# Selective scan on VectorE: scans started from a constant, with a carry step of its own

## The reference, cut to what matters

```
delta = softplus(dts + dt_bias)            # per channel and token
for each token t, in order:                # h: channel x state
    dA = exp(delta[t] * A)                 # A negative, per channel and state
    h  = dA * h + (delta[t] * x[t]) * B[t] # B per state
    y  = sum over states of h * C[t]
out = y + D * x
```

## Time and profile before

| | |
|---|---|
| median of three runs | 24,350.81 us |
| span of the profiled execution | 24,349.2 us |
| time of the profiled execution | not given apart from its span; the fastest run took 24,349.69 us |
| VectorE busy | 23,408.4 us (96%) |
| TensorE busy | 23,475.9 us (96%) |
| ScalarE busy | 22,739.3 us (93%) |
| GpSimd busy | 20,766.4 us (85%) |
| scans in the trace | first start at 3,354.1 us, last at 23,661.3 us |

### The profile page before, as it was taken

One profiled execution on the slowest core, in us unless ns is written; L12 is line 12 of the kernel. 1 busy time (PEld: TensorE's weight loads), 2 busy tenths in 40 slices (PEclk: granted clock), 3 DMA queues, 4 the chain that ended last, 5 costly groups with the idle time before them and its releaser, 6 DMA issues. The chain is left out here.

```text
span 24349.2 us, 520057 instructions
## 1 busy us (share of the span) xinstructions
PE 23475.9 (96%) x197068; PEld 21113.9 (87%) x197068; DVE 23408.4 (96%) x23358; ACT 22739.3 (93%) x45975; POOL 20766.4 (85%) x6924
## 2 busy tenths in 40 slices
PE   5997989999999999999999999999999999999999
PEld 2775469999999999999999899999999999999987
DVE  7998889999999999999999999999999999999996
ACT  4996579999999999999999999999999999999986
POOL 3000049999999999999999999999999999999997
PEclk8998999999999999999999999999999999999999
DMA  5222555555555555555555566666655666666665
GB/s 191 59 64 96 185 184 188 188 186 189 188 186 188 182 189 188 188 190 189 188 188 188 189 193 195 196 194 195 196 194 190 192 199 193 193 198 194 193 200 189
DMA packets 3815249, 4429.59 MB, mean 182 GB/s; under 512 B 2085381, under 2 KB 3140521, under 8 KB 3532585
## 3 DMA queue, kind: packets, MB, share of 16 engines
q1 hardware_dynamic: 3812776, 4396.31, 55.2%
HBM read 3782.68 MB, written 617.09 MB: 181 GB/s over the span
## 5 line engine op out<-in xcount | busy, mean ns | idle before, releaser
L1475 DVE TENSOR_TENSOR_SCAN s_h<-s_da,s_h,s_db 128x512 f32<-128x512 f32 x16256 | 19189.5, 1273 | 86.9 <-PE s_db L1376 86.1
L1493 POOL TENSOR_TENSOR s_prod<-s_h,s_cb 128x2048 f32<-128x2048 f32 x4096 | 18660.9, 4572 | 357.9 <-DVE s_h L1475 289.6
L1445 ACT ACTIVATE s_da<-s_delta,a_neg 128x512 f32<-128x512 f32 x16384 | 10910.5, 718 | 27.0 <-DVE s_h L1475 0.8
L1434 ACT ACTIVATE s_dxb<-s_dx,s_btok 128x256 f32<-128x256 f32 x19328 | 8592.8, 505 | 30.7 <-PEq L63 30.7
L1389 PE MATMUL s_py<-eye,s_prod 128*128 128x128 f32 x65536 | 8498.0, 273 | 15.4 <-POOL s_prod L1493 15.4
L1376 PE MATMUL s_db<-s_bdiag,s_dx 128*128 128x128 f32 x49664 | 8226.6, 275 | 0.0
L1372 PE MATMUL s_db<-eye,s_dxb 128*128 128x128 f32 x40704 | 7232.2, 275 | 309.5 <-ACT s_dxb L1434 299.9
L1389 PEld LDWEIGHTS s_py<-eye,s_prod 128*128 128x128 f32 x65536 | 7435.7, 141 | 19.4 <-POOL s_prod L1493 19.2
L1376 PEld LDWEIGHTS s_db<-s_bdiag,s_dx 128*128 128x128 f32 x49664 | 6839.4, 191 | 0.0
L1372 PEld LDWEIGHTS s_db<-eye,s_dxb 128*128 128x128 f32 x40704 | 4926.4, 141 | 1380.1 <-issue 698.3
L546 POOL COPY a_spread<-a_rden 128x256 f32<-128x256 f32 x256 | 102.8, 402 | 1645.7 <-DVE a_rden L508 1645.7
(11 more groups left out here) (141 smaller groups left out, 16291.9 us busy)
## 6 DMA issues: line engine op xcount, KB each, us to landing
s_cb<-c_rows SPq DMA_DIRECT2D x2048, 1024.0 KB, 5.8
s_bdiag<-b_diag SPq DMA_DIRECT2D x2048, 256.0 KB, 4.9
s_bdiag<-b_diag SPq DMA_DIRECT2D x1536, 192.0 KB, 6.3
y<-s_yt SPq DMA_DIRECT2D x1024, 256.0 KB, 2.7
s_xc<-xc_own SPq DMA_DIRECT2D x384, 512.0 KB, 9.4
s_yb<-y SPq DMA_DIRECT2D x768, 256.0 KB, 4.0
xc_tok<-c_ot SPq DMA_DIRECT2D x32, 2048.0 KB, 7.6
s_xt<-xc_tok SPq DMA_DIRECT2D x256, 256.0 KB, 5.2
```

The costliest lines, as they stand in the source:

```text
L1434: last = e.activation(dxb[:, i % NDXB, j, :], dx[:, g % 2, j, :], ACT.Copy, scale=btok[:, g % 2, 0, j, n:n + 1])
L1445: last = e.activation(da[:, i % NDA, half, :], delta[:, g % 2, half, :], ACT.Exp, scale=wts[k]["a_neg"][:, half, n:n + 1])
L1475: last = e.tensor_tensor_scan(h[:, n, half, flow], da[:, i % NDA, half, flow], db[:, i % NDB, half, flow], first, ALU.mult, ALU.add)
L1493: e.tensor_tensor(prod[:, p % GROUPS_KEPT], h[:, states], columns.unsqueeze(2).to_broadcast([P, TOGETHER, HALVES, T]), ALU.mult).then_inc( ...
```

## The change

Each scan now starts from a constant: 1.0 in every tile but the first of a direction, where it is 0.0 as before. ScalarE writes the exponentials straight into `h` (the buffers `da` are gone), in all tiles but the first only for the 511 tokens after the first in the direction of the scan. VectorE writes the column that is left, by a step of its own (`carry`, a TENSOR_TENSOR of 128x16): the last column of the tile before times `fade`, the exponential of the first token, which ScalarE makes by two small instructions a tile. One carry serves eight states. The carry of states 0 to 7 for the tile to come stands after state 12, that of states 8 to 15 after state 4 of the tile itself.

Delta times x is done by VectorE in all directions (stage `dx`, from PSUM and `xt`), so GpSimd's `double` and ScalarE's copy are gone, and `xt` is loaded everywhere. In directions 2 and 3 `xc` is loaded for one half only. The scalings are shared out by two tables: `WHOLE` names the states with three scaled blocks (the others have two, with a second diagonal, in direction 1 now too), and `POOLED` those whose third block GpSimd scales.

```diff
-    NDA, NDXB, NDB = 3, 3, 2
+    NDXB, NDB = 3, 2
-    ADDED = {1: (5, 9), 2: (8, 11), 3: (8, 11)}
-    SKIPPED = 2
-    SHARE = 2
+    ADDED = {1: (5, 9), 2: (7, 11), 3: (7, 11)}
+    SKIPPED = 1
+    CARRIED = D_STATE // 2
+    CARRY_AT = {12: 0, 4: 1}
-    on_pool = lambda k, n, j: shared(k) and n % SHARE == SHARE - 1 and j == SUBS_ACT - 1
-    second_diagonal = lambda k, n: not shared(k) and n % GROUP != 0 and n != 6
-    scaled_subs = lambda k, n: SUBS_ACT - 1 if second_diagonal(k, n) else SUBS_ACT
+    WHOLE = {0: (0, 1, 4, 6, 8, 12, 15), 1: (0, 1, 2, 4, 6, 8, 10, 12, 14, 15),
+             2: (0, 3, 4, 6, 8, 10, 12, 14), 3: (0, 3, 4, 6, 8, 10, 12, 14)}
+    POOLED = {0: (4, 8, 12), 1: (2, 6, 10, 14), 2: (0, 4, 6, 10), 3: (0, 4, 6, 10)}
+    on_pool = lambda k, n, j: n in POOLED[k] and j == SUBS_ACT - 1
+    scaled_subs = lambda k, n: SUBS_ACT if n in WHOLE[k] else SUBS_ACT - 1
...
-        da = m.sb("s_da", [P, NDA, HALVES, T])
+        fade = m.sb("s_fade", [P, HALVES, D_STATE])
...
-            elif stage == "dx":
-                e.wait_ge(S["turnd"], n)
-                e.copy(flat(dx[:, s]), flat(pr[:, :, :])).then_inc(S["dx"], 1)
+            elif stage == "fade" and tile.t:
+                e.wait_ge(S["delta"], n)
+                if n >= 2:
+                    e.wait_ge(S["carry"], 2 * (n - 1))
+                for half in range(HALVES):
+                    last = e.activation(fade[:, half, :], wts[k]["a_neg"][:, half, :], ACT.Exp,
+                                        scale=delta[:, s, half, first_token(k):first_token(k) + 1])
+                last.then_inc(S["fade"], 1)
...
         PLAN_BACK = {
             "PE": {2: "dts", 9: "turnd"},
-            "ACT": {3: "exp", 4: "log", 10: "dx"},
-            "DVE": {5: "delta"},
-            "POOL": {3: "double"},
+            "ACT": {3: "exp", 5: "log", 7: "fade"},
+            "DVE": {6: "delta", 10: "dx"},
         }
...
-                        if i >= NDA:
-                            scanned(e, i - NDA, HALVES - 1)
+                        if g >= 1 and n % CARRIED == 0:
+                            e.wait_ge(S["carry"], 2 * (g - 1) + n // CARRIED + 1)
                         for half in range(HALVES):
-                            last = e.activation(da[:, i % NDA, half, :], delta[:, g % 2, half, :], ACT.Exp,
+                            last = e.activation(h[:, n, half, later(g)], delta[:, g % 2, half, later(g)], ACT.Exp,
                                                 scale=wts[k]["a_neg"][:, half, n:n + 1])
...
+                    def carry(g, part):
+
+                        if not 1 <= g < TILES:
+                            return
+                        states = slice(part * CARRIED, (part + 1) * CARRIED)
+                        if part == 0:
+                            e.wait_ge(S["fade"], g)
+                        multiplied(e, (g - 1) * D_STATE + (part + 1) * CARRIED - 1)
+                        e.tensor_tensor(h[:, states, :, first_token(k)], h[:, states, :, last_token],
+                                        fade[:, :, states].rearrange("p a n -> p n a"), ALU.mult).then_inc(S["carry"], 1)
+
...
-                        if g >= 1:
-                            multiplied(e, i - D_STATE)
                         for half in range(HALVES):
                             e.wait_ge(S["db"], 2 * i + half + 1)
-                            first = h[:, n, half, last_token:last_token + 1] if g else 0.0
-                            last = e.tensor_tensor_scan(h[:, n, half, flow], da[:, i % NDA, half, flow], db[:, i % NDB, half, flow],
-                                                        first, ALU.mult, ALU.add)
+                            last = e.tensor_tensor_scan(h[:, n, half, flow], h[:, n, half, flow], db[:, i % NDB, half, flow],
+                                                        1.0 if g else 0.0, ALU.mult, ALU.add)
                             last.then_inc(S["h"], 1)
+                        if n in CARRY_AT:
+                            carry(g if CARRY_AT[n] else g + 1, CARRY_AT[n])
                         for coming, stage in due("DVE", g, n):
                             prepare_dve(e, k, coming, stage)
```

More of the change, by code:

```diff
@@ L925, in scans_phase @@
                           "xst0 xst1 xld0 xld1 lowld btl0 btl1 bkeep "
-                          "turned xc proj low turnb btok dts exped log delta doubled turnd dx "
+                          "turned xc proj low turnb btok dts exped log delta fade carry turnd dx "
                           "scaled scaled_pool db da zero zeroed bstore bl0 bl1 bl2 bl3 h prod summed_first summed skipped added y0 y1")
@@ L960, in store_b @@
         def store_b(e, d, t, s):
-            for i in range(diagonals(d)):
+            for i in range(DIAGONALS):
                 there = b_diag[s, i].rearrange("(j m) -> j m", m=D_STATE * P + 1)[:, 0:D_STATE * P]
@@ L1032, in prepare_pe @@
                 e.wait_ge(S["delta"], n)
[L1033 to L1037, removed]
                 for j in range(SUBS):
@@ L1040, in prepare_pe, with first_token @@
                         at = (j % 2) * D_INNER + half * P
-                        last = e.transpose(pr[:, j // 2, at:at + P], source[:, half, j * P:(j + 1) * P], const["eye"][:, :])
+                        last = e.transpose(pr[:, j // 2, at:at + P], delta[:, s, half, j * P:(j + 1) * P], const["eye"][:, :])
                 last.then_inc(S["turnd"], 1)
+        def first_token(k):
+            return T - 1 if backwards(k) else 0
         def consumed(e, k, n):
@@ L1098, in prepare_dve @@
                 e.tensor_tensor(flat(dx[:, s]), flat(pr[:, :, :]), flat(xt[:, s]), ALU.mult).then_inc(S["dx"], 1)
[L1100 to L1105, removed]
         PLAN_KEPT = {
             "PE": {-2: "proj0", 0: "proj1", 3: "turnb", 5: "dts", 11: "turnd"},
-            "ACT": {1: "low", 6: "exp", 7: "log", 12: "dx"},
-            "DVE": {4: "btok", 8: "delta"},
-            "POOL": {4: "double"},
+            "ACT": {1: "low", 6: "exp", 7: "log", 9: "fade"},
+            "DVE": {4: "btok", 8: "delta", 12: "dx"},
         }
@@ L1114, in scans_phase @@
             "PE": {0: "proj0", 1: "proj1", 3: "turnb", 5: "dts", 11: "turnd"},
-            "ACT": {2: "low", 6: "exp", 7: "log", 12: "dx"},
-            "DVE": {4: "btok", 8: "delta"},
-            "POOL": {4: "double"},
+            "ACT": {2: "low", 6: "exp", 7: "log", 9: "fade"},
+            "DVE": {4: "btok", 8: "delta", 12: "dx"},
         }
@@ L1186, in one_direction, with later @@
             last_token = 0 if backwards(k) else T - 1
+            def later(g):
+                if g == 0:
+                    return slice(0, T)
+                return slice(0, T - 1) if backwards(k) else slice(1, T)
             def prepares(g):
@@ L1288, in load_own @@
                             e.wait_ge(S["dx"], t - 2)
-                        e.dma_start(xc[:, t % 2], own(*place(t))).then_inc(S[f"xld{t % 2}"], DMA)
+                        halves = slice(SKIP[place(t)[0]], SKIP[place(t)[0]] + 1) if stored(t) else slice(0, HALVES)
+                        e.dma_start(xc[:, t % 2, halves], own(*place(t))[:, halves]).then_inc(S[f"xld{t % 2}"], DMA)
                     def prefetch(g):
[L1292 to L1295, removed]
+                        if g >= 3:
+                            e.wait_ge(S["dx"], g - 2)
+                        load(e, *place(g), g % 2)
                     prefetch(1)
```

69 lines of the change are left out of this document (31 added, 38 removed).

## The result

| | |
|---|---|
| median after (4 runs) | 26,624.17 us (26,621.96 to 26,628.11) |
| median before, same comparison | 24,350.25 us |
| ratio | 1.0934 [1.0918, 1.0949] |
| predicted | 26,200 us, range 25,400 to 26,700 |

The kernel became 9.3% slower. The time is inside the range given for 8 in 10, 424 us over the predicted value, and 124 us over the likeliest case's own range.

The account below looks back on a forecast made before the run. No engine alone bounds the kernel, VectorE does in direction 0; held carries add 4.60, 4.24, 2.86 and 2.86 us a tile by direction, 14.56 over 127 tiles, 1,849 us on 24,349.2: 26,200 us, range 25,400 to 26,700.

Parts of the forecast that it names:

- the likeliest case: The forecast with carries held and engines waiting for each other: 26,200 us, own range 25,800 to 26,500, 84 in 100.
- The scan in place: VectorE's scans writing over their input from a constant: 1.11 us from one to the next against 1.17, 1.9 us a tile.
- The third rival: Scans in place no faster than now, carries not held: 220 us slower, 24,570 us; chance 2 in 100.
- The carry is held: VectorE's carry, both inputs in SBUF, waits for the rest of GpSimd's product: mean 2 to 4 us long.
- The first rival: The carry on VectorE is not held and costs 0.1 us: 430 us faster, 23,920 us; chance 9 in 100.
- Each engine waits for the other once in half a tile: VectorE waits at the carry, then GpSimd for two scans; GpSimd idle 2 to 3.5 us twice a tile.
- Short waits, the second rival: GpSimd keeps behind, so each carry waits about 1 us: 270 us slower, 24,620 us; chance 5 in 100.
- The mis-sized term: Between carries, VectorE's 17.8 us of work stays under 18.3, so it is always there before GpSimd's product is done.
- the chain: From carry to carry: two scans, GpSimd's start, four GpSimd products, the carry's end; 20.63 us a half, 41.26 a tile.
- The scalings that the prediction counts as visible: GpSimd's scalings not hidden, 0.45 us each: 0.9 us in direction 0, 1.8 in direction 1, 1.35 in 2 and 3.
- VectorE's work without the carry: VectorE's time a tile apart from carries: 38.0 us in directions 0 and 1, 37.8 us in the other two.
- The edits costed at nothing: New `xt` loads, direction 1's second diagonal and two small `fade` instructions: no cost, as they lie beside the chain.

Follow-up runs that it names:

- small_sbuf: The kernel before with one unused 128x16 VectorE product, both inputs in SBUF, added twice a tile: 26,772.33 us, ratio 1.0993.
- small_psum: The kernel before with the same unused 128x16 VectorE product twice a tile, its second input in PSUM: 24,389.1 us, ratio 1.0015.
- nocarry: The changed kernel without its two carry products a tile, so its output is another: 23,901.96 us, ratio 0.9814 against the kernel before.
- carry_13_5: The changed kernel with the carries behind states 13 and 5, not 12 and 4: 25,171.48 us, ratio 1.0336 against the kernel before.
- dx_later: The changed kernel with dx in directions 2 and 3 behind state 11, not 10: 26,388.75 us, ratio 1.0836 against the kernel before.

## Why the prediction was right, and where its number was off

**The scan in place: right.** 1.11 us from one scan to the next, as taken from the first tiles. The third rival falls with it.

**The carry is held: right.** Mean 2.85 us where 2 to 4 was forecast. Each ends 0.04 to 0.05 us behind a product of GpSimd (0.03 forecast). The pair small_sbuf and small_psum shows that for such a product it is the second SBUF input, and not the place, the size or a wait. The first rival, the carry not held, was priced at 23,920 us, and nocarry, which has no carry at all, gave 23,902, so its sum was nearly right and its condition wrong. Tile by tile it had 38.3, 39.9, 38.3 and 38.3 us, measured 38.38, 39.90, 38.25 and 38.24.

**Each engine waits for the other once in half a tile: right.** GpSimd's two gaps a tile are, as medians, 2.15 and 3.54 us in direction 0, 2.41 and 3.54 us in direction 1, and 2.41 and 1.96 us in direction 2. Short waits, the second rival, did not come in the changed kernel. Putting the carry one state later brought them for nearly all carries of directions 0 and 1 and for two thirds of those of directions 2 and 3; the others waited 5.1 us and more (carry_13_5).

**The mis-sized term: "VectorE's seven other states take 7 x 2.22 = 15.5 us of it; with delta and `dx` in the same half 17.8 us, still less than 18.3. So it is always there before the product is done".** By it VectorE adds nothing to the chain between the carries; in directions 2 and 3 it adds 1.4 us a tile. The tiles came out at 43.96, 44.37, 43.95 and 43.95 us against 43.45, 44.17, 42.61 and 42.61: over by 0.51, 0.20, 1.34 and 1.34, together 3.39 us, and over 127 tiles 430 us. That is the whole miss of 424 us. The sum in the quoted step holds for the carry and was not checked for the scans between. In directions 2 and 3 delta stands behind state 6 and dx behind state 10. GpSimd's product of states 6 and 7 therefore waits 0.52 us for a scan, and that of states 10 and 11 0.90 us. From the end of state 5 to the end of state 11 VectorE has twelve scans (13.3 us), delta and dx (2.2 us), 15.5 us in all. In that time GpSimd has three products and one scaling, 13.6 + 0.45 us. So the chain leaves GpSimd and runs over VectorE, which makes it 1.4 us longer a tile. All four waits of GpSimd, 2.41 + 0.52 + 0.90 + 1.96 = 5.79 us, with eight products at 4.53 (36.24) and four scalings at 0.45 (1.8), make 43.83 us; the tile is 43.95. dx_later took 0.93 us a tile away by moving dx alone, in two directions 236 us, and the kernel became 235 us shorter. In direction 0 the product of states 8 and 9 waits 0.47 us in the same way, behind delta. By the order of the instructions the same cause fits there; it was not tried there. What is left in direction 1, 0.20 us, I did not resolve.

**Two sums that do not come out.** The scalings that the prediction counts as visible are 0.9, 1.8 and twice 1.35 us, together 5.4 and not 4.95, so 686 us and not 630; the tile times and the forecast have them right, and only the lower end of the likeliest range was argued from the smaller sum. VectorE's work without the carry adds up to 37.9 and 37.7 us, not 38.0 and 37.8, which changes no result.

**The edits costed at nothing: right as far as the runs tell.** In nocarry, where the chain of waits is gone, direction 1 takes 39.90 us with its second diagonals; the prediction had 39.93 for it. The changed kernel alone could not have shown that, since its chain covers everything.

**The clock.** TensorE's granted clock is 0.97 or 0.98 in the changed kernel, where TensorE idles more, and 1.00 before. The account of the tile just given closes over VectorE and GpSimd alone, to 0.12 us, with instructions as long as before, so TensorE's speed has no visible place in it. No run separates it; in dx_later the clock in directions 2 and 3 was back at 1.00, and the tiles became 0.93 us shorter, about the one wait that dx had caused.

## What to carry to other kernels

Before adding an instruction to VectorE beside a busy GpSimd, count its tensor inputs in SBUF: with two it waits for GpSimd's product to end, even at 16 elements, so give it one input in PSUM, or put it on GpSimd, where 16 elements cost 0.25 us. One input in SBUF and the output there too can be held as well (L1597), so measure it. A busy share does not show such a wait; the mean length of a tiny instruction does. And when two engines hand work back and forth, check every hand-over between the two ends of the chain against the work ahead of it, not the last one alone.

## What the runs showed of the hardware that I had not expected

- When the held instruction is passed over. The Trainium skill (SBUF — State Buffer, Who interferes with whom) calls the ports that the two engines share an exclusive lock. The runs agree: 2,584 ns against 154. What the rows add is that between two products in a row the lock may pass from GpSimd to GpSimd. The carry at 15482.26 was passed over once; it is one of 87 of the 127 behind state 5 in direction 2. In the same kernel other carries were let in between two products in a row: the 40 others there, and 119 of the 127 behind state 5 in direction 1 (median 0.65 us). What decides it stays open.
- One-column instructions with a scalar for each partition were never held for a product, though column and scalar both lie in SBUF (0.59 us at most in 16,256), while L1597 with 32 columns and a constant was. They do cost 0.12 us each in a row, so 16 of them cost 1.93 us, two thirds of one held carry.
- The first value of a scan makes it 0.08 us longer when it is read from SBUF (1,278 ns against 1,198), and this was worth 585 us over the kernel, all of it outside direction 1.
